# One masked move for three, one state copy for sixteen, and a wider norm step in a chunked linear-attention and rail-FFN kernel

## The reference

```python
x = x + layernorm(attn(layernorm(x)))
x = x + layernorm(ffn(layernorm(x)))

# attn: 16 heads of 64 channels, 2 nodes x 32 features per head, causal
q, k, v = split(x @ w_qkv.T + b_qkv)
zn   = z / max(norm(z), 1e-12)                 # z is q or k, per head
proj = einsum('bhtd,rhdm->rbhtm', zn, omega)
feat = proj**2/sqrt(32) * exp(clip(proj*sqrt(2s) - s, -20, 20))/sqrt(32) * sqrt(w)
kv_cum = cumsum(kf * v) + kv_state ; k_cum = cumsum(kf) + k_state
out = (qf . kv_cum) / max(qf . k_cum, 1e-6) ;  out @ w_out.T + b_out

# ffn: y = x_rails @ rail_maker ; z = y @ rail_up ; gelu(z) @ w_cproj.T  (16384 -> 1024)
```

## Time and profile before

| what | value |
|---|---|
| median of 2 runs | 4568.02 us (4558.92 and 4577.13) |
| profiled execution, device time | 4587.82 us |
| span of its slowest core (core 1) | 4586.2 us |
| spans of its 8 cores | 4537.1 to 4586.2 us |
| mean granted TensorE clock of the cores | 0.705 to 0.710 of full speed |
| busy on core 1: TensorE, VectorE, ScalarE | 2279.4, 1155.0, 795.2 us |

### The profile page before, as it was taken

The page is one execution under the profiler, slowest core; times in us unless marked ns, Lnnn a source line. Parts: engine busy times, 40 slices in busy tenths (PEclk is TensorE's granted clock), DMA queues, the critical chain, the costliest instruction groups (busy, mean ns, idle before and its releaser), DMA issues.

```text
span 4586.2 us, 31882 instructions; the slowest of 8 cores (4537.1 to 4586.2 us)
## 1 busy us (share of the span) xinstructions
PE 2279.4 (50%) x10368; PEld 1021.6 (22%) x10368; DVE 1155.0 (25%) x2318; ACT 795.2 (17%) x1161; POOL 51.4 (1%) x73
## 2 busy tenths in 40 slices
PE   1333434344444443434343476666666466666665
PEld 0112222222222222222222122222222122222222
DVE  0333333333333333333333510000001300000003
ACT  0211112211111112121211021111111311111111
POOL 1000000000000000000000000000000000000000
PEclk9666666666666656666665588888777578888887
DMA  7000000000000000000000202222222122222221
GB/s 155 5 10 5 5 10 0 1 0 1 1 0 1 0 0 1 0 1 1 1 0 1 43 14 40 40 41 40 34 32 45 47 37 37 37 37 37 37 37 37
DMA packets 55088, 99.58 MB, mean 22 GB/s; under 512 B 2496, under 2 KB 18880, under 8 KB 53824
## 3 DMA queue, kind: packets, MB, share of 16 engines
q0 software_dynamic: 44880, 80.76, 11.3%
q1 hardware_dynamic: 10048, 16.79, 1.2%
HBM read 169.90 MB, written 8.39 MB: 39 GB/s over the span
## 4 chain that ended last, share of the span: by engine, by line
PE 45%; DVE 24%; DMA 11%; ACT 10%; issue 8%; DVEq 2%; ACTq 1%; POOL 0%; SPq 0%; POOLq 0%
PE psB L812 22%; DMA wc<-wcT 8%; PE psA L397 5%; PE psA L775 3%; DVE oacc L830 3%; PE psA L430 3%; DVE qk_bf L407 2%; PE psB L609 2%; DVEq L83 2%; DMA xa_bf<-x_carry 1%; DVE f32s L318 1%; ACT f32s L323 1%; ACT xa_bf L325 1%; DVE pn_bf L347 1%; PE psA L270 1%
## 5 line engine op out<-in xcount | busy, mean ns | idle before, releaser
L812 PE MATMUL psB<-hsl,wc 128*128 128x512 bf16 x4096 | 1057.7, 405 | 559.7 <-DMA wc<-wcT 439.4
L812 PEld LDWEIGHTS psB<-hsl,wc 128*128 128x128 bf16 x4096 | 375.9, 102 | 1106.0 <-issue 781.8
L786 ACT ACTIVATE hsl<-psA 128x512 bf16<-128x512 f32 x512 | 306.2, 598 | 1359.2 <-PE psA L775 1355.9
L830 DVE TENSOR_TENSOR oacc<-oacc,psB 128x2048 f32<-128x2048 f32 x56 | 128.1, 2288 | 1449.8 <-PE psB L812 1449.8
L397 PE MATMUL psA<-ln_bf,wqkv_bf 128*128 128x256 bf16 x1536 | 253.6, 344 | 86.0 <-DVEq L83 86.0
L264 PE MATMUL psA<-xa_bf,allones_bf 128*128 128x256 bf16 x256 | 58.3, 405 | 382.4 <-DMA xa_bf<-x_carry 217.5
L775 PE MATMUL psA<-ln,railsM 32*128 32x512 bf16 x512 | 210.0, 412 | 22.8 <-DVEq L83 13.6
L585 ACT ACTIVATE f32sB<-f32sB 64x256 f32<-64x256 f32 x128 | 53.2, 416 | 967.6 <-DVEq L83 967.6
L397 PEld LDWEIGHTS psA<-ln_bf,wqkv_bf 128*128 128x128 bf16 x1536 | 185.3, 123 | 149.6 <-issue 92.3
L430 PE MATMUL psA<-wqkv_bf,ln_bf 128*128 128x512 bf16 x512 | 169.7, 505 | 40.1 <-DVEq L83 40.1
L340 PE MATMUL psA<-qk_bf,omega_bf 64*64 64x256 bf16 x384 | 50.9, 413 | 255.1 <-DVEq L83 255.1
(11 more groups left out here) (152 smaller groups left out, 2158.2 us busy)
## 6 DMA issues: line engine op xcount, KB each, us to landing
wc<-wcT POOLq DMA_DIRECT2D x32, 2048.0 KB, 18.0
x_sb<-x_own SPq DMA_DIRECT2D x8, 1024.0 KB, 24.2
y_out<-oacc SPq DMA_DIRECT2D x8, 1024.0 KB, 4.5
wqkv_bf<-wqkvT POOLq DMA_DIRECT2D x8, 768.0 KB, 49.0
xa_bf<-x_carry POOLq DMA_DIRECT2D x8, 512.0 KB, 6.0
wout_bf<-woutT POOLq DMA_DIRECT2D x8, 256.0 KB, 68.4
rut_bf<-rut POOLq DMA_DIRECT2D x4, 128.0 KB, 5.7
omega_bf<-omega POOLq DMA_DIRECT2D x2, 128.0 KB, 15.9
```

The source lines that it names most:

```text
L786: A_((lambda a, fcl=fcl, zsl=zsl, hb=hb: a.activation(hb[:, fcl * 512:(fcl + 1) * 512], psA[:, zsl * 512:(zsl + 1) * 512], AF.Gelu)), wait ...
L812: t.matmul(psB[:, ob * 512:(ob + 1) * 512], wcbufs[fcl // 8][:, (fcl % 8) * 1024 + obi * 128: (fcl % 8) * 1024 + (obi + 1) * 128], hb[:, f ...
L830: V_((lambda v, g=g, obg=obg: v.tensor_tensor(AP(oacc, obg * 4096 + g * 512, [[8 * 1024, 128], [1024, 4], [1, 512]]), AP(oacc, obg * 4096 ...
```

## The change

There are five edits.

1. In a head, the three moves into `ab_bf` become one multiplication of 128 x 384 elements with a mask of 128 x 384, which holds the triangle, ones, and the triangle.
2. The cast of the state to bf16 at the end of each head is taken out. One cast of the whole state, 128 x 528, stands behind the last head of each chunk. For that the state is packed: even and odd heads share columns, on partitions 0 to 63 and 64 to 127, so `S_f` and `S_bf` have 8 x 66 columns in place of 16 x 66. The per-head casts of the carry stage (L490) stay.
3. In `emit_features` the two rounds of 512 columns become one round of 1024, and Ln works in place.
4. `railsM` is allocated at the start, and small attention buffers (`S_bf`, `denrep`, `dinv`, `ab_bf`, the mask, the value bias row and the row of ones) are places in it. The number of loads on the GpSimd queue is the same: the load of the 128 x 128 triangle is gone, that of the 128 x 384 mask is new.
5. The host makes the mask.

Cut to its core:

```diff
-        for sbuf, dr in ((tri_bf, c_tri), (allones_bf, c_allones),
+        for sbuf, dr in ((allones_bf, c_allones),
                          (blockones_bf, c_blockones), (eye_bf, c_eye),
-                         (diagmask_bf, c_diagmask), (bqv_bf, bqv_row)):
+                         (diagmask_bf, c_diagmask)):
             GP((lambda g, a=sbuf, b=dr: g.dma_start(a[:, :], b[:, :])), inc="dw")
+        GP(lambda g: g.dma_start(mask384_bf[:, 0:384], c_mask384[:, :]), inc="dw")
+        GP(lambda g: g.dma_start(railsM[0:1, 384:1408], bqv_row[:, :]), inc="dw")
...
-        ab_bf = sba("ab_bf", (128, 512), BF16)
-        S_f = sba("S_f", (128, 16 * 66), F32)
-        S_bf = sba("S_bf", (128, 16 * 66), BF16)
-        denrep = sba("denrep", (128, 64), BF16)
-        dinv = sba("dinv", (128, 256), BF16)
+        ab_bf = railsM[:, 3424:3808]
+        S_f = sba("S_f", (128, 8 * 66), F32)
+        S_bf = railsM[:, 1856:2384]
+        denrep = railsM[:, 1792:1856]
+        dinv = railsM[:, 1536:1792]
...
-                for qq in range(2):
-                    V_((lambda v, qq=qq: v.tensor_scalar(
-                        f32s[:, 0:512], psA[:, qq * 512:(qq + 1) * 512], 1e-24,
-                        None, op0=ALU.max)),
-                       waits=[("pe", p0)] if qq == 0 else [("ac", P.snap("ac"))])
-                    d1 = P.snap("dv")
-                    A_((lambda a: a.activation(f32s[:, 512:1024], f32s[:, 0:512],
-                                               AF.Ln)), waits=[("dv", d1)])
-                    A_((lambda a, c0=c0, qq=qq: a.activation(
-                        xa_bf[:, c0 + qq * 512:c0 + (qq + 1) * 512],
-                        f32s[:, 512:1024], AF.Exp, scale=-0.5)))
+                V_((lambda v: v.tensor_scalar(
+                    f32s[:, 0:1024], psA[:, 0:1024], 1e-24,
+                    None, op0=ALU.max)), waits=[("pe", p0)])
+                d1 = P.snap("dv")
+                A_((lambda a: a.activation(f32s[:, 0:1024], f32s[:, 0:1024],
+                                           AF.Ln)), waits=[("dv", d1)])
+                A_((lambda a, c0=c0: a.activation(
+                    xa_bf[:, c0:c0 + 1024], f32s[:, 0:1024], AF.Exp, scale=-0.5)))
...
                 V_((lambda v, base=base: v.tensor_tensor(
-                    ab_bf[:, 0:128], psB[:, base:base + 128], tri_bf[:, :],
-                    op=ALU.mult)), waits=[("pe", pa)])
-                V_((lambda v, base=base: v.tensor_copy(
-                    ab_bf[:, 128:256], psB[:, base + 128:base + 256])))
-                V_((lambda v, base=base: v.tensor_tensor(
-                    ab_bf[:, 256:384], psB[:, base + 256:base + 384], tri_bf[:, :],
-                    op=ALU.mult)))
+                    ab_bf[:, 0:384], psB[:, base:base + 384],
+                    mask384_bf[:, 0:384], op=ALU.mult)), waits=[("pe", pa)])
...
                 V_((lambda v, dS0=dS0, hh=hh, lo=lo: v.tensor_tensor(
-                    S_f[lo:lo + 64, 66 * hh:66 * hh + 65],
-                    S_f[lo:lo + 64, 66 * hh:66 * hh + 65],
+                    S_f[lo:lo + 64, 66 * (hh // 2):66 * (hh // 2) + 65],
+                    S_f[lo:lo + 64, 66 * (hh // 2):66 * (hh // 2) + 65],
                     psB[lo:lo + 64, dS0:dS0 + 65], op=ALU.add)))
-                V_((lambda v, hh=hh, lo=lo: v.tensor_copy(
-                    S_bf[lo:lo + 64, 66 * hh:66 * hh + 65],
-                    S_f[lo:lo + 64, 66 * hh:66 * hh + 65])))
                 slot_dv[sl] = P.snap("dv")
+            V_((lambda v: v.tensor_copy(S_bf[:, :], S_f[:, :])))
             scan_done = P.snap("dv")
```

More of the change, by code:

```diff
@@ L120, in build_nc @@
     c_diagmask = dram_in("c_diagmask", (32, 128))
+    c_mask384 = dram_in("c_mask384", (128, 384))
     y_out = nc.dram_tensor("y_out", [DM, NOWN], F32, kind="ExternalOutput")
@@ L129, in build_nc @@
         x_sb = sb("x_sb", (128, DB * NOWN), F32)
+        railsM = sb("railsM", (128, 32 * 128), BF16)
+        mask384_bf = railsM
         omega_bf = sb("omega_bf", (128, 1024), BF16)
         eye_bf = sb("eye_bf", (128, 128), BF16)
-        tri_bf = sb("tri_bf", (128, 128), BF16)
         allones_bf = sb("allones_bf", (128, 128), BF16)
@@ L136, in build_nc @@
         bqkv_sb = sb("bqkv_sb", (128, 16), F32)
-        bqv_bf = sb("bqv_bf", (1, DM), BF16)
         bout_sb = sb("bout_sb", (128, 8), F32)
-        ones_row = sb("ones_row", (1, 128), BF16)
         svecs = sb("svecs", (128, 4), F32)
@@ L190, in build_nc @@
         psT = es.enter_context(nc.psum_tensor("psT", [128, 2048], BF16))
-        V_(lambda v: v.memset(ones_row[:, :], 1.0))
+        V_(lambda v: v.memset(railsM[0:1, 1408:1536], 1.0))
         V_(lambda v: v.memset(eps_c[:, :], EPS))
@@ L439, in stageA_gen @@
                         psA[:, oh * 512:(oh + 1) * 512],
-                        ones_row[0:1, 0:128],
-                        bqv_bf[0:1, oh * 512:(oh + 1) * 512],
+                        railsM[0:1, 1408:1536],
+                        railsM[0:1, 384 + oh * 512:384 + (oh + 1) * 512],
                         start=False, stop=True)))
@@ L490, in stageA_gen @@
                     V_((lambda v, hh=hh, lo=lo: v.tensor_copy(
-                        S_bf[lo:lo + 64, 66 * hh:66 * hh + 65],
-                        S_f[lo:lo + 64, 66 * hh:66 * hh + 65])))
+                        S_bf[lo:lo + 64, 66 * (hh // 2):66 * (hh // 2) + 65],
+                        S_f[lo:lo + 64, 66 * (hh // 2):66 * (hh // 2) + 65])))
         def emit_stageB(ci, parity, pump):
@@ L511, in emit_stageB @@
                     denrep[sl * 64:sl * 64 + 64, 0:64],
-                    AP(S_bf, lo * (16 * 66) + 66 * hh + 64, [[16 * 66, 64], [0, 64]]))),
+                    AP(railsM, lo * 4096 + 1856 + 66 * (hh // 2) + 64,
+                       [[4096, 64], [0, 64]]))),
                    waits=[("dv", slot_dv[sl])])
@@ L541, in emit_stageB @@
                         psB[lo:lo + 64, ctx0:ctx0 + 256],
-                        S_bf[lo:lo + 64, 66 * hh:66 * hh + 64],
+                        S_bf[lo:lo + 64, 66 * (hh // 2):66 * (hh // 2) + 64],
                         qfb[lo:lo + 64, bb * 256:bb * 256 + 256],
@@ L687, in build_nc @@
         es_attn.close()
-        railsM = sb("railsM", (128, 32 * 128), BF16)
         with nc.sbuf_tensor("rmt_bf", [16, 4096], BF16) as rmt_bf, \
@@ L919, in stage_inputs @@
     dmsk[16:, 64:] = 1.0
+    m384 = np.ones((128, 384), np.float32)
+    m384[:, 0:128] = np.triu(np.ones((128, 128), np.float32))
+    m384[:, 256:384] = np.triu(np.ones((128, 128), np.float32))
     shared = dict(wqkvT=wqkvT, bqkv_c=bqkv_c, bqv_row=bqv_row, woutT=woutT,
@@ L923, in stage_inputs @@
                   wcT=wcT, c_eye=c_eye, c_tri=c_tri, c_allones=c_allones,
-                  c_blockones=bo, c_diagmask=dmsk)
+                  c_blockones=bo, c_diagmask=dmsk, c_mask384=m384)
     in_maps = []
```

## The result

The changed kernel takes 4422.59 us in the median of 11 runs (4391.61 to 4482.32), the kernel before 4577.9 us in the median of 10 taken beside it. The ratio is 0.9658, with a 95% interval of 0.9625 to 0.969. The forecast was 4430 us against a median of 4568, a ratio of 0.970. The profiled executions went from 4587.8 to 4429.7 us. Whatever the kernel, in some executions the cores of one die take a few per cent longer at a lower granted clock; the ratios and their intervals leave those executions out, the medians and ranges don't.

The account below looks back on a forecast made before the run. It took hand-offs between engines taking turns as the bound. Mask 72.1, state cast 22.9 and features 43.7, less 0.7 for the mask load, made 138 us: 4430 us from a median of 4568, range 4378 to 4483.

Parts of the forecast that it names:

- What bounds the kernel: Attention: TensorE, VectorE and ScalarE mostly take turns, 212 of 222 us in a main chunk; only instructions in the chain count.
- The mask: Moves into `ab_bf`, 128 heads: 1.122 us become one move of 0.559, gaining 72.1 us; bounds 55 and 106.
- third rival: Behind the merged move into `ab_bf`: gap 0.29 us in place of 0.13, 21 us lost, 4451 us; chance 0.03.
- The state cast: End of heads: 78 casts on the path, 24.8 us, less 1.9 for the new 434 ns cast; net 22.9 us.
- count by pieces: Head-end state casts: 9 on the path in each of 7 chunks with pieces, 15 in the last, 78 in all.
- The features: `emit_features`, 48 halves: 4.60 us becomes 3.69, gaining 43.7 us in all; 17 us if only hand-offs go.
- Edits at nothing: Matmuls, carry-stage casts and places in `railsM` bring no change; the larger mask load costs 0.7 us.
- The FFN keeps its time: FFN stage, with no changed instruction: keeps its 2062 us.
- first rival: Clock holds longer in seven heads of seven chunks, 31 us, and output projections, 19 us more: 4380 us; chance 0.11.
- bounds of the terms: Whole kernel: all terms at lower ends gain 85 us, 4483 us; at upper ends 185 us, 4383 us.

Follow-up runs that it names:

- x_hidden: Changed kernel plus four unread 64x65 casts behind heads 1, 2, 4, 5, 7 and 8 of chunks 0 to 6, under TensorE passes; ratio to kernel before 0.9631.
- x_exposed: Changed kernel plus the same 168 added casts behind heads 9 to 14 of chunks 0 to 6, where no pass runs; ratio to kernel before 0.9782.
- u_state: Changed kernel with the state cast behind every head put back and the one 128x528 cast taken out; ratio to kernel before 0.9698.
- u_all: Changed kernel with all three instruction edits undone, leaving the packed state and the places in `railsM`; ratio to kernel before 1.0001.
- u_mask: Changed kernel with the three moves into `ab_bf` put back; ratio to kernel before 0.988.
- d2: Changed kernel plus two 64x65 casts ahead of the state cast, once in each of 8 main chunks; attention done at 2366.6 us.
- d8: Changed kernel plus eight 64x65 casts ahead of the state cast, once in each of 8 main chunks; attention done at 2376.4 us.
- carry_pack: Changed kernel with one 128x520 addition for 16 in each carry chunk, and one cast at the stage's end for 16 per chunk; ratio to kernel before 0.9509.

## Why the prediction was right, step by step

- *What bounds the kernel*: right. The chain of hand-offs was shortened, and neither another engine nor a transfer took its place: the gain of the plain last chunk was 13.9 us for 13.6 forecast.
- *The mask*: the instruction was sized to 1 ns (558 for 559). What undoing it costs, 89 us, is more than its 72; the 17 beyond are for the larger part TensorE's busy time (10.2 us in chunks 1 to 6).
- *The gap behind a longer instruction* (third rival): wrong. The context matmul starts 1404.63 - 1404.46 = 0.17 us behind the end of the 558 ns move. In the kernel before it started at 2401.70, 0.18 us behind the end of the last 292 ns move, which stands below. The flush of the Trainium skill (VectorE: DVE Perf Modes, The DRAIN you can't avoid) is for the next VectorE operation, and it isn't seen there either: behind a VectorE instruction of 1.23 us the next one starts after 0.12 us (1431.67 - 1431.55, the second and third row). The rows, from the timeline of the kernel before and from that of the changed one:

```profile
2401.23 0.29 DVE L534 TENSOR_TENSOR ab_bf<-psB,tri_bf 128x128 bf16<-128x128 f32 x1
```

```profile
1430.32 1.23 DVE L296 TENSOR_TENSOR ctx_bf<-qf_a,mrB 128x2048 bf16<-128x2048 bf16 x1 [1.18 <-ACTq L83]
1431.67 1.23 DVE L298 TENSOR_TENSOR ctx_bf<-ctx_bf,mrB 128x2048 bf16<-128x2048 bf16 x1
```

- *The state cast*: the count by pieces holds. `x_hidden` and `x_exposed` gave 3 and 52 us where 0 and 53 were expected, and the new cast took 434 ns. Its net of 23 us was read as 17 in `u_state`, in which TensorE happened to be 4.8 us less busy in chunks 1 to 6.
- *The features*: 3.69 us a half, as forecast; undoing them cost 49 us for 44.
- *Edits at nothing*: right. `u_all` is at 1.0001 of the kernel before. The larger mask load can't be seen: the first load of `x_carry` starts at 62 to 63 us in the changed kernel and at 65 in the kernel before.
- *The FFN keeps its time*: 2037 and 2019 us in the mean of the cores, 2045 before and 2020 in `u_all`. It holds within its own unevenness. On the slowest cores it is 2062 before and 2060 after, the latter with the stretches at 0.81.
- *The clock* (first rival, 4380 us): half of its place was right and its size was not. The seven heads behind the value passes stayed at the low level: VectorE's wait for them fell from 246 to 242 us in all 128 heads, not by 31. The output projections got 7 us less in all, where it had 19. The value passes, which the rival left out, gave 5 us more in chunks 1 to 6. Its reason, shorter idling ahead of the burst, is refuted by `u_mask` and by `d2` to `d8`.
- The term that was missing in the sum is thus about 20 us on 138: 15 us of TensorE's busy time in chunks 1 to 6, 4 open in the carry stage, and small change. The attention ended at 2368 us on core 3, the slowest, where 2386 was forecast. The range held this easily, since the bounds of the terms alone gave some 50 us on either side. That the median lies only 7 us from 4430 is in part luck: the kernel before had 4577.9 us beside it and not 4568, and the fall is 155 us and not 138.

## What to carry to other kernels

Where the timeline shows engines taking turns, cost each edit from duration plus gap, and count only the places where no longer work of another engine lies over it; the straight line through two rows of other widths gives the duration of a merged instruction to a nanosecond. When one merged instruction is worth it, look for the same pattern elsewhere: here the packed state made a second saving possible, in the carry stage, as large as the largest of the three edits made. And treat 10 to 20 us of a 4500 us kernel like this as movable by TensorE's clock alone: over the kernels here its busy time in the same six chunks lay between 526 and 549 us. Compare it before a difference of that size is put down to an edit.

## What the runs showed of the hardware

- With more idle time ahead of it, a burst of 64 matmuls became slower, slower still, and faster again: 68.7, 75.2, 77.7 and 73.7 us for eight bursts with 26.0, 31.1, 36.8 and 45.7 us of idling ahead of them.
- The Trainium skill (TensorE: Matmul & The Clock Gate, What you observe and HAM oscillation) has the moment of the rise vary from run to run, and idling as what brings the clock down. Here it largely repeats over cores and executions: the kernel before and `u_all` have the same eight moments, 4.3 to 5.2 us into the projection, within 0.3 us on all cores. It can differ from chunk to chunk (2.6 to 5.8 us in `d2`), and it moves when the length of a chunk changes.
- A granted clock of 0.81 that is neither level was held for stretches in three of the thirteen profiled executions, on some cores only.
- VectorE's instructions with fp32 input from PSUM lie on one line whether they have a second operand or not: 292, 558, 692 and 1225 ns at 128, 384, 512 and 1024 columns. The addition of 128x520 in `carry_pack`, with an fp32 operand in SBUF, took 0.70 us and lies on it as well.
